# Causal mask of the row maxima in an attention kernel: added by VectorE in PSUM instead of by four bf16 products of TensorE

## The reference, cut to what matters

```
q, k, v = LN(x) @ Wq + bq, ...          # 16 heads of 64
q, k = rope(q), rope(k)
attn = softmax(where(tril, q @ k.T / 8, -inf))
x = LN(x + (attn @ v) @ Wo + bo + x)
x = LN(x + (silu(x @ Wg.T) * (x @ Wu.T)) @ Wd.T)   # Wg, Wu, Wd are int32 times 1/127
```

## Time and profile before

| | |
|---|---|
| time, median of 3 runs | 2189.78 us (2185.9 to 2190.99) |
| the profiled execution's own time | 2190.48 us |
| its span | 2188.7 us |
| mean granted clock of PE | 0.986 of full speed |
| busy: PE, DVE, POOL, ACT | 95%, 71%, 64%, 42% of the span |
| products of line 1205 | 1024, 60.3 us busy in all |

### The profile page before, as it was taken

The page is one execution under the profiler, slowest core; times in us unless marked ns, Lnnn a source line. Parts: engine busy times, 40 slices in busy tenths (PEclk is TensorE's granted clock), DMA queues, the critical chain, the costliest instruction groups (busy, mean ns, idle before and its releaser), DMA issues.

```text
span 2188.7 us, 38909 instructions
## 1 busy us (share of the span) xinstructions
PE 2073.8 (95%) x15488; PEld 1311.4 (60%) x15488; DVE 1549.2 (71%) x2181; ACT 915.9 (42%) x1262; POOL 1401.2 (64%) x1206
## 2 busy tenths in 40 slices
PE   6889999999999999999999999999999989999997
PEld 5555555555555555555555555555555545788986
DVE  7577767676778776767767777767777765666654
ACT  4434343444343434434344444443444344534442
POOL 3368777777787876677878787878787878100000
PEclk9899999999999999999999999999999999999999
DMA  6411212121212122122121212121112131222200
GB/s 207 132 44 46 57 42 61 38 65 35 61 32 63 33 74 69 46 67 68 44 59 44 59 44 59 44 59 34 49 35 55 34 131 44 76 93 75 98 10 29
DMA packets 116154, 132.25 MB, mean 60 GB/s; under 512 B 15248, under 2 KB 71184, under 8 KB 115728
## 3 DMA queue, kind: packets, MB, share of 16 engines
q1 hardware_dynamic: 115984, 129.92, 20.1%
HBM read 56.47 MB, written 39.85 MB: 44 GB/s over the span
## 4 chain that ended last, share of the span: by engine, by line
PE 68%; DVE 20%; DMA 3%; issue 3%; SPq 3%; ACT 2%; POOL 1%; ACTq 0%; DVEq 0%
PE o_ps L1261 15%; DVE mpart L875 8%; PE m_ps L1200 8%; PE s_ps L1221 5%; PE s_ps L1225 4%; PE s_ps L1227 4%; PE s_ps L1223 4%; PE x_ps L1155 3%; DMA rot<-qr 3%; SPq L387 3%; DVE qc L902 3%; PE x_ps L1243 3%; PE x_ps L1268 2%; PE x_ps L1157 2%; PE x_ps L1156 2%
## 5 line engine op out<-in xcount | busy, mean ns | idle before, releaser
L561 POOL TENSOR_TENSOR acc<-acc,pt 128x512 f32<-128x512 f32 (+3 forms) x1024 | 1199.1, 1204 | 209.5 <-ACT pt L615 209.1
L875 DVE TENSOR_REDUCE mpart<-m_ps 128x2 f32<-128x1024 f32 (+2 forms) x576 | 625.0, 1085 | 309.6 <-PE m_ps L1200 227.4
L615 ACT ACTIVATE pt<-s_ps 128x1024 f32<-128x1024 f32 (+3 forms) x640 | 544.3, 896 | 701.4 <-PE s_ps L1227 334.3
L1261 PE MATMUL o_ps<-pt,v 128*64 128x512 f32 (+3 forms) x2560 | 538.1, 541 | 0.0
L1200 PE MATMUL m_ps<-qk 64*128 64x512 f32 (+3 forms) x1280 | 288.1, 446 | 62.6 <-DVE mpart L875 52.9
L1200 PEld LDWEIGHTS m_ps<-qk 64*128 64x128 f32 x1280 | 120.7, 185 | 367.9 <-DVE mpart L875 211.4
L1261 PEld LDWEIGHTS o_ps<-pt,v 128*64 128x64 f32 x2560 | 159.7, 137 | 222.6 <-issue 202.6
L556 POOL TENSOR_TENSOR acc<-pt 128x512 f32<-128x512 f32 (+1 forms) x128 | 166.8, 1325 | 160.5 <-ACT pt L615 160.5
L1221 PE MATMUL s_ps<-qk 64*128 64x512 f32 (+3 forms) x1280 | 253.4, 392 | 0.0
L1225 PE MATMUL s_ps<-qk 64*128 64x512 f32 (+3 forms) x1280 | 234.7, 362 | 0.0
L1227 PE MATMUL s_ps<-aux,ones_r 64*128 64x512 f32 (+3 forms) x1280 | 234.7, 362 | 0.0
(11 more groups left out here) (168 smaller groups left out, 2883.1 us busy)
## 6 DMA issues: line engine op xcount, KB each, us to landing
rot<-qr SPq DMA_DIRECT2D x512, 64.0 KB, 2.0
attn<-o_sum SPq DMA_DIRECT2D x64, 256.0 KB, 2.3
o_raw<-attn SPq DMA_DIRECT2D x8, 2048.0 KB, 9.0
v<-v_far SPq DMA_DIRECT2D x16, 768.0 KB, 5.3
v_far<-v_part SPq DMA_DIRECT2D x48, 256.0 KB, 2.0
w_raw<-in_wqkv SPq DMA_DIRECT2D x34, 128.0 KB, 4.8
v_far<-v SPq DMA_DIRECT2D x16, 256.0 KB, 2.6
v<-v_far SPq DMA_DIRECT2D x16, 256.0 KB, 4.5
```

The source lines that it names most:

```text
L561: nc.gpsimd.tensor_tensor(sums, sums, probs, ALU.add).then_inc(summed, 1)
L615: nc.scalar.activation(pt[:, u % SLOTS, :, q0:NB], s_ps[:, two:two + 2, q0:NB], ACT.Exp, scale=SCALE)\
L875: nc.vector.tensor_reduce(dst, m_ps[:, :, 0:w], AX.X, ALU.max, negate=True).then_inc(maxed, 1)
L1261: last = nc.tensor.matmul(o_ps[rows, q0:NB], v[par][:, j, rows], pt[:, u % SLOTS, a, q0:NB], start=(j == 0), stop=(j == n - 1), skip_group ...
```

## The change

PE no longer adds the mask to `m_ps`; DVE does, with one addition in place over the diagonal 128 columns of both banks, before it reduces the unit. The addition takes the unit's wait for PE, and the reduction waits for the addition by a new semaphore. The mask tensor holds one whole 128 x 128 mask for that in place of two half masks.

```diff
-        mask_b = sb("mask_b", [P, 4, P], BF16)
+        mask_b = sb("mask_b", [P, 3, P], BF16)
+        m_masked = sem("m_masked")
...
                 dst = mc[:, t // TG, t % TG, :] if parts == 1 else mpart[:, t % 2, :, c]
+                if c == parts - 1:
+                    own = m_ps[:, :, w - P:w]
+                    nc.vector.tensor_tensor(own, own, mask_b[:, 2, :].unsqueeze(1).broadcast_to([P, 2, P]),
+                                            ALU.add).then_inc(m_masked, 1)
+                    dve.wait_ge(m_masked, n * TT + (t + 1))
                 nc.vector.tensor_reduce(dst, m_ps[:, :, 0:w], AX.X, ALU.max, negate=True).then_inc(maxed, 1)
...
-                diag = c == t // TG
                 for a, rows in enumerate(halves):
                     last = nc.tensor.matmul(m_ps[:, a, 0:w], qk[par][rows, 0, q], qk[par][rows, 1, k],
-                                            start=True, stop=not diag)
-                if diag:
-                    for x in range(2):
-                        for a, rows in enumerate(halves):
-                            last = nc.tensor.matmul(m_ps[:, a, w - P + DK * x:w - P + DK * (x + 1)],
-                                                    mask_b[rows, 2 + x, :], id_b[rows, :], start=False, stop=x == 1)
+                                            start=True, stop=True)
                 last.then_inc(m_scored, 1)
```

More of the change, by code:

```diff
@@ L460, in _ @@
             for dst, src in ((sin_sb[:, :], sin), (cos_sb[:, :], cos),
-                             (mask_b[:, :, :], masks[:, 0:4 * P].rearrange("p (m n) -> p m n", m=4)),
-                             (id_b[:, :], masks[:, 4 * P:4 * P + DK]), (b_v[:, :], bv),
+                             (mask_b[:, :, :], masks[:, 0:3 * P].rearrange("p (m n) -> p m n", m=3)),
+                             (id_b[:, :], masks[:, 3 * P:3 * P + DK]), (b_v[:, :], bv),
                              (bo_sb[:, :], bo.partition_broadcast(P))):
@@ L1508 @@
     r, k = np.arange(P)[:, None] % DK, np.arange(P)[None, :]
-    masks = [np.where(later, np.float32(MASKED), np.float32(0))
-             for later in (k > r, k > r + DK, r > k, r + DK > k)]
+    row = np.arange(P)[:, None]
+    masks = [np.where(later, np.float32(MASKED), np.float32(0)) for later in (k > r, k > r + DK, k > row)]
     def with_first(a, n):
```

## The result

The changed kernel takes 2245.82 us (median of 4 runs, 2240.0 to 2249.21) against 2190.39 us for the kernel before in the same comparison: a ratio of 1.0253, 95% interval 1.024 to 1.0266, or 55 us more. Forecast were 2222 us, 32 more. The direction was right and the time lies in the range of 2200 to 2250, but near its upper end, and outside the 2210 to 2235 that the forecast's own mechanism was given.

The account below looks back on a forecast made before the run. PE was taken to bound the kernel, with frequent handovers where DVE is last. Exposed delays of 2.55 us per pair less 0.55 saved give 2.0, times 16 is 32 us: 2190.5 + 32 - 0.7 = 2222 us, range 2200 to 2250.

Parts of the forecast that it names:

- The bound, and DVE's place in it: Whole kernel: bound by PE, 95% busy, with frequent handovers of `m_ps` in which DVE is last; 20% of chain on DVE.
- PE's saving per unit, 0.07 us: From a 512-column maxima unit to the next scores product: 0.34 us without mask, 0.41 with; 18 us over 256 units.
- More than that PE can't give back: On PE: dropping the mask products of 256 diagonal units saves at most 18 us.
- I keep half: PE's saving of 1.1 us a pair: part ahead of handovers where DVE is last is swallowed, so 0.55 us counts.
- The addition, 0.44 + 0.04 us: DVE's mask addition takes 0.44 us and the reduction's wait 0.04 more: 0.48 us per diagonal unit, 123 us in all.
- The exposed delays, 2.55 us per pair, 41 us: At `m_ps` handovers with too little cover, mainly tiles 2, 3, 4, 6, 7, 11, 13, 14, DVE's delay reaches PE: 2.55 us per pair.
- With 0.85 for an addition beside POOL: Upper bound for DVE's new addition, from an all-SBUF addition beside POOL: at least 51 us more loss, 2273 us.
- Rival 1: DVE sets the pace and delays add up; 133 late diagonal units pay 0.48 us in full: 2245 us, chance 0.18.
- Rival 3: The reduction's wait for the addition is free, so 0.48 becomes 0.35 us, 16 us less: 2206 us, chance 0.08.

Follow-up runs that it names:

- the covered and uncovered tiles: Changed kernel with DVE masking only tiles 0, 1, 5, 8, 9, 10, 12, 15, or only the other eight, PE the rest: 2185.38 and 2255.19 us.
- POOL idle: Kernel before and changed kernel, each with POOL's row sum additions cut to 16 columns and sums filled with ones: 2132.09 and 2145.64 us.
- the run of the moved entries: Changed kernel and kernel before, each with a low part and a division moved later in DVE's list, behind maxima units: 2254.98 and 2228.65 us.

## Why the prediction was right, and where it was off

- **The bound, and DVE's place in it.** Right. PE with handovers in which DVE is last; the covered and uncovered tiles, told apart by the time from the reduction's end to PE's next start, did what the rows said: 0.9967 against 1.0288.
- **PE's saving per unit, 0.07 us.** Read rightly from rows 6, but too small as the saving. The next product does start 0.07 us earlier without the mask (19 us in all), yet where scores follow, the one after it starts another 0.08 us earlier, which makes 29 us in all and 0.11 us per unit. "More than that PE can't give back" was wrong: 24 us were given back. The rule of the Trainium skill, "VectorE: DVE Perf Modes", section "The TRN2 errata", which the prediction set aside, gives 0.117 us per unit and 30 us in all, an estimate that comes out near these 29. The trace doesn't disagree with it, as the prediction said; only the interval up to the very next product does.
- **"I keep half" of the saving.** This step failed. It was a guess between two bounds. Alone, 24 of 29 us arrive at the end; beside the additions nothing of it can be seen (2241.51 with PE's products, 2245.82 without). The 9 us that the sum put down for it are neither.
- **The addition, 0.44 + 0.04 us.** Right: 0.421 us, and with the wait the reduction starts 630.13 - 629.70 = 0.43 us later than the addition, which took 0.40 there.
- **The exposed delays, 2.55 us per pair, 41 us.** The mechanism was right and the size too small: 4.4 us per pair, 70 us. With POOL idle it is 2.1 us, and 0.56 against 0.54 behind tile 3. The term that was mis-sized is DVE's other work: I let every other DVE instruction keep its length. The largest misses are the places where they did not: +0.80 us behind tile 3, where the low part went from 0.68 to 1.45 us (medians of the place here and in what follows), +0.73 us at tile 12, where nothing was forecast and the division went from 0.94 to 1.78, and +0.38 us at tiles 6 and 7, where the low part went from 0.79 to 1.62. These three make 1.9 us per pair, about the whole difference between 2.55 and 4.4. Elsewhere lengths fell (the low part behind tile 8 from 1.43 to 1.04 us), where PE did not wait for them.
- **"With 0.85 for an addition beside POOL".** I had the row that should have warned: line 902 with a mean of 1.105 us beside reductions that hardly vary (0.65 to 0.69 us for those of 512 columns). I read it as a price for the new instruction, which has one input in PSUM and doesn't pay it, and not as a price that depends on the moment for the old ones.
- **Rival 1** gave 2245 us, the measured time, by another road: all 133 late units paying in full. That is not what happened. With the covered tiles left on DVE the stalls rose by 7 us only, and with POOL idle most of the loss was gone. That the time lies in the stated range is in part luck: the upper part of the range stood there for this rival, whose mechanism the runs don't show, and the two errors of the forecast itself, 29 us too little stall and 20 us too little saving by PE, work against each other; the rest of the miss is the 6 and 6.5 us of other steps of PE, for which the sum had no term. The rival's general point, that DVE's list has little room, fits the run of the moved entries.
- **Rival 3**, a wait that costs nothing, is not supported: it gave 2206, further from the measured time than the forecast, and the reduction did start behind the addition's end.
- **PE's clock** adds a little. Columns of the windows are PE, PEld, DVE, ACT and POOL busy, clock, DMA share and GB/s; before, and after:

```profile
120.00:230.00 110.00, 104.95 (x810) 61.44 (x806) 81.16 (x103) 45.30 (x59) 79.95 (x69) 1.00 0.18 49
```
```profile
120.00:230.00 110.00, 100.95 (x700) 58.31 (x700) 80.68 (x109) 42.57 (x57) 74.79 (x66) 0.95 0.15 42
```

In the first pair of the changed kernel, where PE idles more, the granted clock was 0.95, so for a tenth of the window it was at 1.2 GHz instead of 2.4. Before it was 1.00 there. Over the whole span the mean fell from 0.986 to 0.983. No run isolates what that cost. In the sum of PE's starts above, 6.5 us are left over for it and everything else; 3.9 of them lie between 100 and 200 us of the span.

## What to carry to other kernels

Before work is given to an engine with idle time, look at who waits for that engine: for each handover read the time from the end of its instruction to the start of the next user, and give it work only where that time is longer than the work. Then look which of its instructions have lengths that vary in the profile. In this kernel those depended on what ran beside them, and a delay of half a microsecond doubled some of them. To price a saving, compare the starts of several products behind it, not only of the next one. A saving on the busiest engine should be counted together with the delay that pays for it, never by itself.

## What the runs showed of the hardware

The lengths of DVE's instructions with two SBUF inputs (low part, division, second step of rope) follow POOL closely. In the kernel before 259 of these 312 begin inside a POOL addition that has 0.06 us or more to run. Their length is then the rest of that addition plus 0.55 us, with nearly no spread: the median is 0.547 to 0.549 us for each of the three lines, and all but the outermost tenths lie between 0.546 and 0.552. Four of them lie above 0.60, one at 1.78, where POOL's next addition ran as well. The other 53 take 0.68 to 0.70 us, but for one of 1.01. After the change 255 begin inside one, and 0.549 us holds again. So DVE doesn't share with POOL: all but some 0.14 us of its 0.69 us comes after the end of POOL's addition. Where DVE begins first, as at 607.10 above, it keeps its 0.68 us, and POOL pays: in the kernel before 198 additions of 512 columns begin inside such a DVE instruction. Their length is the rest of it plus 1.14 us (all but the outermost twentieths between 1.12 and 1.16), 1.73 us as the median, where an addition that meets none takes 1.29 us. The one at 607.58 above is such a case: 0.20 us and 1.14 make its 1.34. Instructions with one input in PSUM and one in SBUF don't show it: of the 256 new additions 178 begin inside a POOL addition and take 0.419 us as the median, and line 898 stands at 0.739 us on average.

The Trainium skill, "SBUF — State Buffer", section "Who interferes with whom", says that a DVE instruction with two SBUF inputs contends with a GpSimd instruction that reads SBUF, and one with at most one SBUF input, outside the two-port performance modes, doesn't. The trace agrees with both, and shows the price for `tensor_tensor`: the rest of POOL's addition and 0.55 us, by the numbers above.

A kernel that beats both is the one with seven tiles on DVE, 2177.72 us. The one with no mask in the maxima is faster still, 2168.82 us. There the shift that is taken from the scores is the maximum over hidden keys as well. A shift common to a row cancels in the softmax, but where a hidden score lies far above all the visible ones of its row the visible exponents can underflow. No run explored such inputs, so its use beyond these is open.
